# Code-book search of a fused convolution kernel: when VectorE picks the candidate blocks, for pixel chunks 1 to 5

## The reference, cut to what matters

```
z_flat = gn(x) as (4608 pixels, 128)
d = sum(z_flat**2) + sum(codebook**2) - 2 * z_flat @ codebook.T
idx = argmin(d, axis=1)
z_q = codebook[idx]
x = x + (z + (z_q - z))          # z = gn(x)
```

## Time and profile before

| what | value |
|---|---|
| median of 3 runs | 1628.95 us (1627.26 to 1629.37) |
| span of the profiled execution, first to last instruction | 1625.7 us |
| median less span (launch and end, outside of the profile) | 3.25 us |
| TensorE, VectorE busy over the span | 74%, 83% |
| ScalarE, GpSimd busy over the span | 27%, 63% |

### The profile page before, as it was taken

The page is one execution under the profiler, slowest core; times in us unless marked ns, Lnnn a source line. Parts: engine busy times, 40 slices in busy tenths (PEclk is TensorE's granted clock), DMA queues, the critical chain, the costliest instruction groups (busy, mean ns, idle before and its releaser), DMA issues. The chain is left out here.

```text
span 1625.7 us, 19842 instructions
## 1 busy us (share of the span) xinstructions
PE 1203.1 (74%) x6050; PEld 749.5 (46%) x6094; DVE 1347.6 (83%) x1880; ACT 432.4 (27%) x1363; POOL 1027.7 (63%) x983
## 2 busy tenths in 40 slices
PE   5898999799888998888856676576655566545565
PEld 2454555344444444444445454454444344434444
DVE  5578898799999999898858989997787777888776
ACT  1241000124443343252456231221212211111111
POOL 6169798614443343136777677777777777777773
PEclk9889999799999999999978897787777867766777
DMA  5041000011211111054466797787877878777774
GB/s 170 14 154 55 1 0 0 15 48 44 59 55 44 34 46 55 5 172 133 147 219 190 224 289 208 210 270 228 249 208 229 251 229 250 209 234 210 210 209 145
DMA packets 111102, 232.65 MB, mean 143 GB/s; under 512 B 14676, under 2 KB 60500, under 8 KB 110748
## 3 DMA queue, kind: packets, MB, share of 16 engines
q0 software_dynamic: 58176, 191.30, 39.7%
q1 hardware_dynamic: 52828, 40.17, 7.8%
HBM read 205.15 MB, written 26.26 MB: 142 GB/s over the span
## 5 line engine op out<-in xcount | busy, mean ns | idle before, releaser
L2147 POOL DMA_INDIRECT code_region<-corners,lead_region x252 | 242.0, 960 | 77.9 <-issue 75.2
L1927 DVE SCALAR_TENSOR_TENSOR max_region<-score,nc,max_region 128x512 f32<-128x512 f32 x324 | 231.2, 742 | 33.3 <-PE score L1481 31.2
L772 POOL TENSOR_TENSOR prod_acc<-prod_acc,prod_pool 128x768 f32<-128x768 f32 (+8 forms) x118 | 172.0, 1457 | 61.5 <-DVE prod_pool L747 52.6
L2147 POOL DMA_INDIRECT early_region<-corners,lead_region x136 | 129.1, 949 | 41.3 <-issue 40.5
L1518 PE MATMUL score<-ident,code_region 128*128 128x128 f32 x540 | 95.7, 338 | 78.5 <-DVE code_region L1984 74.0
L2147 POOL DMA_INDIRECT max_region<-corners,lead_region x130 | 123.6, 951 | 41.3 <-issue 38.7
L2147 POOL DMA_INDIRECT late_region<-corners,lead_region x126 | 119.4, 948 | 43.2 <-issue 37.5
L1927 DVE SCALAR_TENSOR_TENSOR max_region<-lead_score,nc,max_region 128x512 f32<-128x512 f32 x180 | 132.5, 743 | 8.9 <-PE lead_score L1481 8.2
L1518 PEld LDWEIGHTS score<-ident,code_region 128*128 128x128 f32 x540 | 78.0, 175 | 94.9 <-DVE code_region L1984 87.8
L2062 POOL DMA_INDIRECT late_region<-code_rows,block_id x35 | 35.9, 1026 | 135.3 <-DVE block_id L1765 99.0
L1980 DVE TENSOR_TENSOR lead_score<-lead_score,code_region 128x768 f32<-128x768 f32 x78 | 75.4, 966 | 38.9 <-DMA code_region<-corners,lead_region 35.8
(11 more groups left out here) (298 smaller groups left out, 3089.0 us busy)
## 6 DMA issues: line engine op xcount, KB each, us to landing
corners<-lead_region SPq DMA_DIRECT2D x72, 192.0 KB
corners<-lead_region SPq DMA_DIRECT2D x8, 576.0 KB
code_rows<-codes_n SPq DMA_DIRECT2D x8, 516.0 KB, 3.8
codes_t<-in_codes_t SPq DMA_DIRECT2D x8, 512.0 KB, 3.7
codes_n<-in_codes SPq DMA_DIRECT2D x8, 512.0 KB, 4.1
code_region<-corners,lead_region POOLq DMA_INDIRECT x252, 3.7
x<-in_x SPq DMA_DIRECT2D x2, 1152.0 KB, 6.4
out<-x SPq DMA_DIRECT2D x4, 576.0 KB, 3.1
```

The lines of the kernel that those rows point to most:

```text
L772: pool.tensor_tensor(to, to, v, ALU.add).then_inc(pooled, 1)
L1927: dve.scalar_tensor_tensor(r, score[SLOT[k]], nc2[:, m:m + 1], r, ALU.add, ALU.max).then_inc(dve_took, 1)
L2147: pool.indirect_dma_start(quad(T, k), None, table[j].rearrange("n s c -> n (s c)"), bass.IndirectOffsetOnAxis(index[j % B][:, at:at + 1], 0))\
```

## The change

It applies to chunks 1 to 5 (`SPREAD`). In them find and place of tiles 0 and 1 stand in step one after units 2, 4, 9, 11, those of tiles 2 and 3 in step two after units 2, 4, 9, 11; the fine pairs begin at (2, 6), (2, 13), (3, 4), (3, 11). GpSimd's order is rewritten. `turn_zq` and `subtract_z` go from the end of step three to units 3 and 5 of the next chunk's step zero. In chunk 6 some `lead` steps move by one to three units.

```diff
--- before.py
+++ after.py
@@ -1101,6 +1101,8 @@
     LOWER_FROM, LOWER_ADDED = 0, (10, 19, 28)
     TURN_AT = 9, 11
     Z_TURN_AT = 12
+    SPREAD = range(1, EARLY + 1)
+    ZQ_TURN_AT, SUBTRACT_AT = 3, 5
     SLOT = [0, 1, 2, 3, 0, 4, 1, 2, 0, 3, 4, 1, 0, 2, 3, 4]
 
     LAST = [max(j for j in range(k - NPR, k) if SLOT[j % NPR] == SLOT[k]) for k in range(NPR)]
@@ -1437,9 +1439,9 @@
             def lead(n, s, k):
 
                 at = n - L0, s, k
-                if at == (0, 0, 13):
+                if at == (0, 0, 15):
                     depthwise.pe_norm(pe, 0, lead_ps)
-                if at == (0, 1, 6):
+                if at == (0, 1, 7):
                     depthwise.pe_kernels(pe, 0, lead_ps)
                 tap = (s - 2) * NPR + k - LOWER_FROM
                 if n == L0 and 0 <= tap < NCH // 2 * TAPS:
@@ -1483,8 +1485,10 @@
                         turn(S - 1, TURN_AT.index(k))
                     if k == Z_TURN_AT and n and s == 0:
                         turn_z(n)
+                    if k == ZQ_TURN_AT and s == 0 and n - 1 in SPREAD:
+                        turn_zq(n - 1)
                     lead(n, s, k)
-                if n and s == STEPS - 1:
+                if n and s == STEPS - 1 and n not in SPREAD:
                     turn_zq(n)
 
             def norm(m):
@@ -1868,14 +1872,14 @@
             def lead(n, s, k):
 
                 at = n - L0, s, k
-                if at == (0, 0, 10):
+                if at == (0, 0, 12):
                     dve.wait_ge(x_added, 1 + 2 * EARLY)
                     depthwise.norm.dve_moments(dve, x[:, 0, :])
-                if at == (0, 0, 15):
+                if at == (0, 1, 2):
                     depthwise.norm.dve_group(dve, 0, lead_ps[:, 0:ImageNorm.PS])
-                if at == (0, 1, 3):
+                if at == (0, 1, 4):
                     depthwise.dve_pool(dve, 0)
-                if at == (0, 1, 11):
+                if at == (0, 1, 12):
                     depthwise.dve_kernels(dve, 0, lead_ps)
                 for t, when in enumerate(((0, 2, 2), (0, 2, 6), (0, 2, 8), (0, 2, 12), (0, 2, 15),
                                           (0, 3, 5), (0, 3, 8), (0, 3, 10), (0, 3, 13))):
@@ -1906,6 +1910,11 @@
                 if at == (2, 1, 14):
                     weigh(0, 1, 1)
 
+            spread_parts = {(1, 2): (find, 0), (1, 4): (place_block, 0), (1, 9): (find, 1), (1, 11): (place_block, 1),
+                            (2, 2): (find, 2), (2, 4): (place_block, 2), (2, 9): (find, 3), (2, 11): (place_block, 3),
+                            **{(s, k + i): (part, u)
+                               for s, k, u in ((2, 6, 0), (2, 13, 1), (3, 4, 2), (3, 11, 3))
+                               for i, part in enumerate((fine_find, fine_place))}}
             parts = {(0, 12): (find, 0), (0, 14): (place_block, 0), (1, 2): (find, 1), (1, 4): (place_block, 1),
                      (1, 6): (find, 2), (1, 8): (place_block, 2), (1, 10): (find, 3), (1, 12): (place_block, 3),
                      **{(s, k + i): (part, u)
@@ -1926,11 +1935,14 @@
                     r = run[s % 2][k % 2]
                     dve.scalar_tensor_tensor(r, score[SLOT[k]], nc2[:, m:m + 1], r,
                                              ALU.add, ALU.max).then_inc(dve_took, 1)
-                    if n and (s, k) in parts:
-                        part, u = parts[s, k]
+                    when = spread_parts if n in SPREAD else parts
+                    if n and (s, k) in when:
+                        part, u = when[s, k]
                         part(n, u)
+                    if k == SUBTRACT_AT and s == 0 and n - 1 in SPREAD:
+                        subtract_z(n - 1)
                     lead(n, s, k)
-                if n and s == STEPS - 1:
+                if n and s == STEPS - 1 and n not in SPREAD:
                     subtract_z(n)
 
             def norm(m):
@@ -2098,6 +2110,24 @@
             def step(n, s):
                 if not n:
                     return
+                if n in SPREAD:
+                    if s == 1:
+                        gather(n, 0)
+                        multiply(n, 0)
+                        gather(n, 1)
+                    if s == 2:
+                        multiply(n, 1)
+                        gather(n, 2)
+                        fetch(n, 0)
+                        gather(n, 3)
+                        multiply(n, 2)
+                        fetch(n, 1)
+                    if s == STEPS - 1:
+                        multiply(n, 3)
+                        fetch(n, 2)
+                        fetch(n, 3)
+                        add(n)
+                    return
                 last = n == NPX - 1
                 if last and s == 0:
                     rows(APART, range(5))
```

## The result

The changed kernel takes 1674.64 us, median of 4 runs (1666.74 to 1680.95), against 1628.11 us before: a ratio of 1.0285, 95% interval 1.026 to 1.031. Forecast were 1667 and a range of 1657 to 1675, slower. The profiled execution has a span of 1674.9 us, 49.2 more than before; the runs scatter over 14 us where the 4 of before lie within 3 (29 later runs of before spread over 9.7 us, 1623.03 to 1632.71).

The account below looks back on a forecast made before the run. VectorE was taken as busiest, 48.09 of 51.09 us a chunk, with TensorE setting plain steps. -0.6 + 5 x 6.23 + 4 x 0.06 + 2.5 = +33.3, plus 5 for the clock, +38.3 on 1628.95: 1667 us, range 1657 to 1675.

Parts of the forecast that it names:

- the clock term: TensorE at half clock after the new wait in chunks 1 to 5: 1.0 us each, +5, bounds 0 and +8.5.
- chunk 6: Extra turn and subtraction in step zero, lead steps later, diagonals delayed: +2.5 us, bounds +1 to +4.
- VectorE's idle 3.0 us: VectorE's idle time in a 51.09 us chunk of 1 to 5, taken as the most that could be won.
- The chain of 7.66 us behind place 3: Gather 3, multiply 2, ScalarE's sum and unit hold VectorE before unit 2 of step three: 4.8 us lost.
- The late sum of tile 0: ScalarE sums until 14.3, delaying its unit 0 of step two to 15.0: VectorE loses 1.1 us.
- Step three: TensorE sets its pace after the long wait: 10.6 us of work and 0.2 for the hand-over.
- The fetch: Fetch after the last fine place is tighter; TensorE waits 0.2 to 0.3 us in the next chunk's step zero.
- The moved turn: TensorE's turn, 0.44 us, moved to the next step zero: 12.37 us against 12.31, +0.06.
- the second rival: The clock falls fully at all five stalls: 33.3 + 8.5, 1671 us; chance 0.20.
- Not slower: Rival: ScalarE reaches step three in time, so VectorE's idle 3.0 us a chunk can go: 1616 us; chance 0.03.
- The 52.1 us of a chunk with nothing late: Steps of 14.2, 14.4, 11.2 and 12.3 us in chunks 1 to 5 if no queue holds anything.
- Multiply 2 is not held: Rival: gather 3's wait passes earlier, so chunks take 52.1 us: +7, 1636 us; chance 0.05.

Follow-up runs that it names:

- experiment 1: The changed kernel with multiply 2 put ahead of gather 3 on GpSimd in step two: 1652.46 us, ratio 1.015 to before.
- the best placement found: The kernel before with only find and place of tile 3 moved to step two in chunks 1 to 5: 1624.7 us, ratio 0.9975.
- experiment 4: The changed kernel with 16 unread matmuls on TensorE after unit 3 of step three in chunks 1 to 5: 1663.62 us, ratio 1.0231.
- experiment 2: The changed kernel with finds, fine pairs and GpSimd's order put back; moved turn, subtraction and lead steps stay: 1629.12 us, ratio 1.0005.
- experiment 8: The kernel before with only chunk 6's lead steps at the changed kernel's units: 1630.8 us, ratio 1.0018.
- experiment 5: The changed kernel, multiply 2 ahead of gather 3, ScalarE's units ahead of sums 0 and 2, fine pairs, turn, subtraction shifted: 1649.64 us, ratio 1.0139.
- experiment 3: The changed kernel with chunk 6's lead steps back at their old units: 1667.48 us, ratio 1.025.

## Why the prediction was right, and where it was not

The mechanism was right and is shown by experiment 1; the size of the clock term and of chunk 6 was not, and the number stayed in the range by luck.

**What bounded the kernel**, VectorE's idle 3.0 us as all there was to win: nothing contradicts it, and the best placement found wins 0.65 of it. That no placement wins more is not shown.

**The chain of 7.66 us behind place 3** measured 7.54, its wait 4.71 for 4.8. **The late sum of tile 0** ahead of step two: VectorE waited 1.13 for 1.1. Step by step in chunk 2: 15.08, 19.07, 12.44 and 12.31 us against 15.0, 19.25, 10.8 and 12.4. Step three is the only one off, and experiment 4 gives it 10.75 at full clock. **The fetch**, 0.2 to 0.3 us of waiting, fits step zero's 12.31; in chunk 5 TensorE waited 0.92 us for it and step zero took 13.25, and 13.14 in experiment 4, which I had not foreseen. **The moved turn** at no cost: shown by experiment 2.

**The clock was mis-sized.** I took +5 us with +8.5 as the bound. Without it the sum for chunks 1 to 5 is -0.6 + 31.15 + 0.24 = 30.8; measured are 42.6, so up to 11.8 us are the clock's, 0.9 of them rather chunk 5's fetch. Experiment 4, which fills the waits, takes 9.4 us off the five chunks. Two things failed. First, all five long waits brought the clock down, as the second rival had it, where my 1.0 for each was an average over stalls with and without the loss. The Trainium skill, "TensorE: Matmul & The Clock Gate", Part 1, states that the throttled state is the default and that activity releases it. The five falls agree with that; a stretch of 10.3 us at 0.50 in chunk 6, in which TensorE was busy for 9.33 (below), could not have been told from it. Stretches of the changed kernel with their clock, one in step one and then the five of step three:

```profile
365.70:369.10 3.40, 3.40 (x9) 1.20 (x10) 1.87 (x3) 2.87 (x17) 1.74 (x3) 0.50 0.29 51
389.60:393.00 3.40, 3.36 (x8) 1.22 (x8) 2.79 (x8) 2.46 (x16) 0.63 (x3) 0.50 0.01 2
447.60:451.00 3.40, 3.40 (x9) 1.22 (x8) 2.91 (x7) 2.78 (x17) 0.93 (x1) 0.50 0.00 0
505.60:509.00 3.40, 2.66 (x7) 1.01 (x8) 2.23 (x4) 2.78 (x15) 1.85 (x1) 0.51 0.07 19
563.70:570.50 6.80, 4.94 (x12) 1.79 (x13) 3.88 (x8) 4.83 (x27) 3.32 (x4) 0.50 0.04 10
625.10:631.90 6.80, 5.29 (x13) 1.94 (x14) 3.88 (x8) 4.49 (x25) 3.32 (x4) 0.50 0.03 10
```

Second, my bound was no bound. The low stretches of chunks 4 and 5 last 6.8 us, not 3.4, and 365.70 lies in step one, behind an idle time of only 1.69 us:

```profile
365.65 0.61 PE L1481 MATMUL lead_score<-early_region,code_region 128*128 128x512 bf16 x1 [1.69 <-DVE max_region L1936]
```

I had read from 1.62 us at a clock of 1.00 that such waits do nothing. In the changed kernel the same wait of 1.69 us in step one went with a low clock in chunks 1, 4 and 5 and without one in chunks 2 and 3; four more waits of 1.69 us, in step two, brought none.

**Chunk 6 was mis-sized too**: +2.5 forecast, bounds +1 to +4, +7.3 measured. All but 0.4 of it lies in step one: steps two and three take 21.56 and 22.14 us in both kernels. Step one before, in the changed kernel, and in experiment 1, whose code of chunk 6 is that of the changed kernel, and then chunk 6 of experiments 1 and 4:

```profile
617.53:638.14 20.61, 14.83 (x70) 8.02 (x70) 17.68 (x31) 10.40 (x36) 7.99 (x9) 0.92 0.28 78
656.72:684.25 27.53, 20.11 (x74) 11.54 (x74) 18.34 (x36) 10.98 (x38) 10.22 (x9) 0.75 0.21 58
639.89:663.26 23.37, 17.18 (x78) 9.37 (x78) 18.25 (x35) 10.65 (x36) 8.57 (x9) 0.89 0.23 68
622.06:706.96 84.90, 72.07 (x310) 38.05 (x315) 73.17 (x122) 25.23 (x93) 23.22 (x22) 0.94 0.10 29
629.32:714.25 84.93, 72.14 (x309) 37.96 (x315) 73.27 (x121) 25.23 (x93) 23.17 (x22) 0.94 0.10 29
```

In the changed kernel TensorE waited 4.31 us for the pooled mean and then ran at 0.50 for 10.3 us, where before it waited 3.15 and ran low for 3.4; in experiment 1 it waited 2.58. So 3.0 of the 7.3 us come and go with identical code, together with where the low clock falls. That is the clock again, and I had left it out of this chunk's sum.

```profile
662.60:672.90 10.30, 9.33 (x33) 6.58 (x35) 7.02 (x12) 2.90 (x2) 5.61 (x4) 0.50 0.18 51
```

Before scatters in the same way: its code of chunk 6 took 80.64 us in one profile and 83.75 and 82.66 in others (the last with a filler), so the profile of before was at the short end. The medians give 2.4 us for the moved lead steps (experiment 8), with an interval from 0.2 to 5.5. How the other 4.3 us divide between the work moved in and the clock is not shown.

**The two errors of size point the same way**, 6.8 and 4.8 us, so the sum of +38.3 is 11.6 under the 49.9 of the profile. That the number counts as inside the range is luck: the median of 1674.64 lies 0.4 us under its end, two of the four runs lie above it, and as a growth, +46.5, it is over the +45.8 from which the end was worked out, since the four runs of before have a median 0.8 us lower than the one that I added to. What happened at the five stalls is the second rival, to which I gave 0.20 and 1671.

**The rivals.** "Not slower" is excluded, and not only by the chain: with the queues ahead of them cleared (experiment 5) steps one and two still lose. The 52.1 us of a chunk with nothing late came out in no run, so it stays an estimate. "Multiply 2 is not held" did not happen by itself; made by hand (experiment 1) it gave 1652 and not 1636. Its chunk 4, at a clock of 1.00 throughout, took 54.52 us and not 52.1, and 1.7 of these 2.4 us are VectorE's waits for ScalarE's units, 1.13 and 0.59: I had left the late sum of tile 0 out of that rival's chunk. The other chunks lost more, three of them with a low clock (0.90 in step one of chunk 2), and chunk 6 took 84.90.

## What to carry to other kernels

Moving work within one engine moves what is queued behind it on the others: before a find is put later, follow its result through each queue in the order written, up to the next instruction on the engine that the stage waits for, and compare that chain with the work that can still cover it. Here it was 7.5 us against 2.8, and one swapped pair of instructions was worth 22 us. A wait on TensorE is to be priced with what the clock does behind it. And an even split of load is no aim in itself: work is best put where the engine would idle, and the end of step zero was such a place.

## What the runs showed of the hardware that was not expected

The granted clock of TensorE, full or half, came low around waits of 4.0 us (five of five, and again five of five in experiment 3). It also did at three of five waits of 1.69 us that are alike in the program, and at a wait of 3.02 us early in chunk 6 in experiments 1 and 4 but not in the changed kernel, with identical code. It stayed low for 3.4, 6.8 or 10.3 us. TensorE was busy for 9.33 of those 10.3. So identical code takes different times: chunk 6 of before 80.6 or 83.8 us, that of the changed kernel 84.9 or 87.9, and the changed kernel's runs 1666.7 to 1680.9. Filling the wait of 4 us in each of five chunks with unread matmuls brought the total down by 11 us; filling the 3.15 us wait in chunk 6 did nothing that could be told, and there the clock came low at another wait behind it. What decides whether a short wait does so was not settled.
